# The gate of the second half: first layer on every partition, second layer as a row sum on DVE

## What is computed

```python
pooled = hidden_states.mean(axis=1)
h1 = jax.nn.relu(pooled @ gate_w1.T + gate_b1)          # 256 -> 64, per batch
base_act = jax.nn.sigmoid(h1 @ gate_w2.T + gate_b2)     # 64 -> 1
mod = jax.nn.sigmoid(safety_score[:, None] / TEMPERATURE)
strength = (base_act * mod * knob)[:, None, :]
...
return hidden_states + strength * response
```

## Time and profile before

| | |
|---|---|
| median of 3 runs | 1390.7 us (1389.85 to 1391.23) |
| profiled execution | 1390.32 us, its span 1388.2 us |
| busy: PE, DVE, ACT, POOL | 1335.7 (96%), 1066.6 (77%), 1077.6 (78%), 870.3 us (63%) |
| mean granted TensorE clock | 0.989 |
| part of the chain that ended last on PE | L1374 14%, L1361 14%, L1407 3%, L1385 1%, L1391 1%, L1396 1% |

### The profile page before, as it was taken

How to read it: one execution, slowest core, us unless ns; L and a number is a source line. 1 busy time by engine, 2 the same in 40 slices (tenths; PEclk the granted TensorE clock), 3 DMA queues, 4 the chain that set the end, 5 groups by cost and what they waited for, 6 DMA issues and landing times. The chain is left out here.

```text
span 1388.2 us, 39650 instructions
## 1 busy us (share of the span) xinstructions
PE 1335.7 (96%) x11998; PEld 1126.6 (81%) x11998; DVE 1066.6 (77%) x3539; ACT 1077.6 (78%) x2696; POOL 870.3 (63%) x874
## 2 busy tenths in 40 slices
PE   3899999999999999999999998799999999999997
PEld 3677777777777777777777776499999999999997
DVE  3787787777777877887777777577888888787875
ACT  0788888888888888888888887677777777777773
POOL 3989989999999998998998997222122122222210
PEclk9999999999999999999999999989999999999999
DMA  7656555565565564564654671001111111101000
GB/s 229 211 165 200 170 185 188 167 197 177 168 206 167 176 208 155 189 202 150 200 192 154 223 225 33 26 29 32 45 30 32 44 30 38 37 30 45 30 24 32
DMA packets 182766, 175.01 MB, mean 126 GB/s; under 512 B 15648, under 2 KB 182208, under 8 KB 182720
## 3 DMA queue, kind: packets, MB, share of 16 engines
q1 hardware_dynamic: 182720, 174.42, 39.5%
HBM read 157.63 MB, written 16.78 MB: 126 GB/s over the span
## 5 line engine op out<-in xcount | busy, mean ns | idle before, releaser
L423 POOL TENSOR_TENSOR ring<-ring,maskv 128x1024 f32<-128x1024 f32 x256 | 600.0, 2371 | 14.9 <-DMA ring<-in_fside 7.6
L885 ACT ACTIVATE ring<-ring,nmax 128x256 f32<-128x256 f32 x1024 | 453.0, 502 | 28.4 <-DVE nmax L599 28.4
L599 DVE CUSTOM_DVE_ANT_0 ring<-bank,ring 128x256 f32<-128x256 f32 x1024 | 373.1, 418 | 91.2 <-PE bank L1150 74.9
L890 ACT ACTIVATE pT<-bank 128x512 f32<-128x512 f32 x416 | 239.5, 592 | 101.6 <-PE bank L1165 101.5
L1165 PE MATMUL bank<-ident,ring 128*128 128x128 f32 x2048 | 293.5, 279 | 1.4 <-ACT pT L890 1.1
L1165 PEld LDWEIGHTS bank<-ident,ring 128*128 128x128 f32 x2048 | 232.3, 143 | 70.7 <-issue 47.8
L1020 ACT ACTIVATE work<-bank,b1t 128x256 f32<-128x256 f32 x256 | 107.5, 475 | 117.7 <-PE bank L1361 117.7
L1361 PE MATMUL bank<-hT_high,w_high 128*128 128x256 f32 x512 | 154.4, 302 | 4.2 <-DVE hT_rest L771 4.2
L1150 PE MATMUL bank<-work 32*128 32x256 f32 x2048 | 148.3, 404 | 5.2 <-DVE nmax L599 5.2
L1374 PE MATMUL bank<-w_high,gT_high 128*128 128x256 f32 x512 | 148.1, 289 | 0.0
L455 POOL TENSOR_SCALAR vpeb<-mvb 128x2 f32<-128x2 f32 x32 | 6.1, 191 | 226.5 <-DVE mvb L686 226.2
(11 more groups left out here) (158 smaller groups left out, 2724.3 us busy)
## 6 DMA issues: line engine op xcount, KB each, us to landing
ring<-in_fside SPq DMA_DIRECT2D x128, 1024.0 KB, 7.5
xt<-in_x SPq DMA_DIRECT2D x32, 256.0 KB, 3.1
x_d<-x2s SPq DMA_DIRECT2D x32, 256.0 KB, 7.7
work<-x_d SPq DMA_DIRECT2D x32, 256.0 KB, 2.7
out<-pT SPq DMA_DIRECT2D x32, 256.0 KB, 2.2
mk<-in_mask SPq DMA_DIRECT2D x32, 64.0 KB, 6.5
w<-in_W SPq DMA_DIRECT2D x2, 1024.0 KB, 10.5
wada<-in_W_ada SPq DMA_DIRECT2D x1, 512.0 KB, 4.3
```

The source lines that it names most:

```text
L423: nc.gpsimd.tensor_tensor(v, v, m, ALU.add).then_inc(s_masked, 1)
L599: nc.vector.tensor_tensor_reduce(out=v, in0=score_ps[h % HG][:, qt], in1=v, scale=-1.0, scalar=ROW_MAX_NEG, op0=ALU.add, op1=ALU.min, accu ...
L885: nc.scalar.activation(v, v, ACT.Exp, bias=nmax[:, b.par, h, qt:qt + 1], scale=-1.0).then_inc(s_exp, 1)
L890: nc.scalar.activation(pT[:, h % (2 * HG)], tp_ps[h % 2], ACT.Copy).then_inc(s_pta, 1)
```

## The change

Both layers of the gate give their result on all 128 partitions. The first layer now takes `pooled`, a column repeated to 128x128, as weights and moves the 64 columns of `gw1`: h1 lies along a row, the same row on every partition. DVE adds the bias (`gate_hidden`), and a second DVE instruction (`gate_sum`) applies relu, multiplies with the row `gw2` and sums along the row into `zsum`. `gate_z` on TensorE and `gate1` on ACT are gone. `gb1` and `gw2` are loaded as rows on every partition. On TensorE `up_pair(b, 1)` now stands ahead of `y_transpose`, and `hid_transpose` waits for h1 instead of z before it overwrites bank 6.

```diff
-gb1 = sb("gb1", [GW, 1]); gw2 = sb("gw2", [GW, 1])
+gb1 = sb("gb1", [P, GW]); gw2 = sb("gw2", [P, GW])
-h1 = sb("h1", [GW, 1])
+h1 = sb("h1", [P, GW]); h1w = sb("h1w", [P, GW]); zsum = sb("zsum", [P, 1])
...
-            (gb1[:], gate_b1.rearrange("(p a) -> p a", a=1)), (gw2[:], gate_w2T), ...
+            (gb1[:], gate_b1.partition_broadcast(P)), (gw2[:], gate_w2T.rearrange("p a -> (p a)").partition_broadcast(P)), ...
...
+            def gate_hidden(b):
+                dve.wait_ge(s2_h1p, b.n + 1)
+                nc.vector.scalar_tensor_tensor(h1[:], bank[6][:, 0:GW], 1.0 / S, gb1[:], ALU.mult, ALU.add).then_inc(s2_h1, 1)
+
+            def gate_sum(b):
+
+                dve.wait_ge(s2_h1, b.n + 1)
+                if b.i is not None or b.off >= 1:
+                    dve.wait_ge(s2_z, b.n)
+                dve.nop(nofuse=True)
+                nc.vector.scalar_tensor_tensor(h1w[:], h1[:], 0.0, gw2[:], ALU.max, ALU.mult, accum_out=zsum[:]).then_inc(s2_zs, 1)
...
                 if tail2:
+                    gate_hidden(b.plus(-2))
+                    gate_sum(b.plus(-2))
                     rsp_out(b.plus(-2))
...
-            def gate1(b):
-                act.wait_ge(s2_h1p, b.n + 1)
-                nc.scalar.activation(h1[:], bank[6][0:GW, 0:1], ACT.Relu, bias=gb1[:], scale=1.0 / S).then_inc(s2_h1, 1)
-
             def gate2(b):
-                act.wait_ge(s2_zp, b.n + 1)
+                act.wait_ge(s2_zs, b.n + 1)
                 if b.i is not None or b.off >= 1:
                     act.wait_ge(s2_str, b.n)
-                nc.scalar.activation(gth[:], bank[6][:, 8:9], ACT.Tanh, bias=gb2h[:], scale=0.5).then_inc(s2_z, 1)
+                nc.scalar.activation(gth[:], zsum[:], ACT.Tanh, bias=gb2h[:], scale=0.5).then_inc(s2_z, 1)
...
             def hid_transpose(b):
                 pe.wait_ge(s2_hid, b.n + 1)
                 if b.i is not None or b.off >= 1:
-                    pe.wait_ge(s2_z, b.n)
+                    pe.wait_ge(s2_h1, b.n)
...
             def gate_h1(b):
                 pe.wait_ge(s2_hidf, b.n + 1)
                 for c in range(DC):
-                    ins = mm(bank[6][0:GW, 0:1], gw1[:, c], pooled[:, c:c + 1], start=(c == 0), stop=(c == DC - 1))
+                    ins = mm(bank[6][:, 0:GW], pooled[:, c:c + 1].to_broadcast([P, P]), gw1[:, c], start=(c == 0), stop=(c == DC - 1))
                 ins.then_inc(s2_h1p, 1)
-
-            def gate_z(b):
-                pe.wait_ge(s2_h1, b.n + 1)
-                mm(bank[6][:, 8:9], h1[:].to_broadcast([GW, P]), gw2[:], start=True, stop=True).then_inc(s2_zp, 1)
...
                 if main:
                     up_pair(b, 0)
+                    up_pair(b, 1)
                     if n is None or n + 1 < B:
                         y_transpose(b.plus(1))
-                if main:
-                    up_pair(b, 1)
                 if tail2:
                     gate_h1(b.plus(-2))
...
-                if tail2:
-                    gate_z(b.plus(-2))
```

More of the change, by code:

```diff
@@ L138, in attention_block_kernel @@
         scr = sb("scr", [P, B]); modh = sb("modh", [P, B]); modt = sb("modt", [P, B])
-        gw1 = sb("gw1", [P, DC, GW]); gb1 = sb("gb1", [GW, 1]); gw2 = sb("gw2", [GW, 1]); gb2 = sb("gb2", [P, 1]); gb2h = sb("gb2h", [P, 1])
+        gw1 = sb("gw1", [P, DC, GW]); gb1 = sb("gb1", [P, GW]); gw2 = sb("gw2", [P, GW]); gb2 = sb("gb2", [P, 1]); gb2h = sb("gb2h", [P, 1])
         uv = sb("uv", [P, 2, DC, R]); ucol = sb("ucol", [P, 2, DC]); gsb = sb("gsb", [P, 2, R]); gii = sb("gii", [P, 2])
@@ L197, in attention_block_kernel @@
         fin = carve(2, QT, D)
-        pooled = sb("pooled", [P, DC]); h1 = sb("h1", [GW, 1]); gth = sb("gth", [P, 1]); strg = sb("strg", [P, 2])
+        pooled = sb("pooled", [P, DC]); h1 = sb("h1", [P, GW]); h1w = sb("h1w", [P, GW]); zsum = sb("zsum", [P, 1]); gth = sb("gth", [P, 1]); strg = sb("strg", [P, 2])
         st6b = sb("st6b", [P, QT, 6]); mvb = sb("mvb", [P, 2, QT, 2]); vpeb = sb("vpeb", [P, QT]); rstdb = sb("rstdb", [P, QT]); mnegb = sb("mnegb", [P, QT]); nmrb = sb("nmrb", [P, QT])
@@ L229, in attention_block_kernel @@
         s2_yt = sem("s2_yt"); s2_hT = sem("s2_hT"); s2_up = sem("s2_up"); s2_th = sem("s2_th"); s2_u = sem("s2_u"); s2_ua = sem("s2_ua"); s2_w = sem("s2_w"); s2_wl = sem("s2_wl"); s2_hf = sem("s2_hf"); s2_hl = sem("s2_hl"); s2_gh = sem("s2_gh"); s2_gl = sem("s2_gl"); s2_hidf = sem("s2_hidf"); s2_hidl = sem("s2_hidl"); s2_m = sem("s2_m"); s2_ml = sem("s2_ml"); s2_g = sem("s2_g"); s2_dn = sem("s2_dn")
-        s2_hid = sem("s2_hid"); s2_hidp = sem("s2_hidp"); s2_hidT = sem("s2_hidT"); s2_r = sem("s2_r"); s2_h1p = sem("s2_h1p"); s2_h1 = sem("s2_h1"); s2_zp = sem("s2_zp")
+        s2_hid = sem("s2_hid"); s2_hidp = sem("s2_hidp"); s2_hidT = sem("s2_hidT"); s2_r = sem("s2_r"); s2_h1p = sem("s2_h1p"); s2_h1 = sem("s2_h1"); s2_zs = sem("s2_zs")
         s2_z = sem("s2_z"); s2_str = sem("s2_str"); s2_rs = sem("s2_rs"); s2_fin = sem("s2_fin")
@@ L251, in attention_block_kernel @@
             (gw1[:], gate_w1T.rearrange("(c p) n -> p c n", p=P)),
-            (gb1[:], gate_b1.rearrange("(p a) -> p a", a=1)), (gw2[:], gate_w2T), (gb2[:], gate_b2.partition_broadcast(P)),
+            (gb1[:], gate_b1.partition_broadcast(P)), (gw2[:], gate_w2T.rearrange("p a -> (p a)").partition_broadcast(P)), (gb2[:], gate_b2.partition_broadcast(P)),
             (respT[:], resp_wT),
@@ L1076, in body2 @@
                     gT_high(b, 0)
-                if tail2:
-                    gate1(b.plus(-2))
                 if main:
```

## The result

The changed kernel took 1373.65 us (median of 4 executions, 1371.87 to 1374.12) against 1390.85 us (4 executions): ratio 0.9876, 95% interval 0.9861 to 0.9891. A later series of 4 gave a median of 1372.8 (1371.27 to 1374.35), ratio 0.9867 (0.9837 to 0.9896), against a median of 1389.6 for the kernel before in that series. So it is faster by some 17 us, near the forecast of 1372.0 and inside its range. The profiled execution took 1371.87 us (span 1369.7).

What follows compares the result with a forecast made beforehand. TensorE's own instruction stream was taken as the bound, 14.71 us a pass. Gains 29 x 0.60 = 17.4, pass 31 0.5, pass 0 0.6, end 0.2 sum to 18.7 us: 1372.0 us, range 1369 to 1378.

Steps and rivals of the forecast that it cites:

- gate_z, 0.50 us: Gate's second layer on TensorE: removing it gains 0.50 us a pass, though its records take 0.31 on the chain.
- gate_h1, 0.41 us from the Gram product: Gate's first layer on TensorE: four records at the Gram product's 0.1025 each, 0.41 us; gain 0.10 with the transposes.
- rival 1: Gate_h1's edges stay, caused by f32 with a wait, not shape; gate_h1 costs 0.59, time 1377.3 us; chance 0.12.
- slow exit back to the ordinary products: TensorE after y's transposes: a delay before ordinary products resume, taken as already contained in the transposes' 0.44 us.
- The loads and the edges: Gate_h1 on TensorE: four records grow from 0.33 to 0.41 us, and the edges of 0.18 vanish with the shapes.
- a sum 3.8 us worse: Gate_h1's weight loads: by the skill's rule four loads cost 0.21 us more instead of 0.08, worsening the whole sum.
- Pass 0, 0.6 us: Start of the second half: second up pair ends 0.85 us sooner with the order exchanged; counted as 0.6 us.
- DVE hidden: New gate_hidden and gate_sum, 0.75 us of DVE's queue, fit narrowly in 0.89 us: nothing on the path.
- it costs 1:1 once it is over 1.6 us: DVE's new work: beyond room of 0.89 + 0.7 us, each added us lengthens the path by as much.
- Rival 2: DVE's work not fully hidden: 2.0 us per pass stalls hid transposes 0.4; gain 7, about 1385 us; chance 0.06.
- rival 3: Slower than before: gate_sum holds up DVE; needs 2.3 us for both instructions; 2.5 gives 1398 us; chance 0.03.
- The end, 0.2 us: Last output: strength can follow rsp_out directly, 0.6 us behind, without gate_z and its tanh; gain 0.2 us.

Runs made afterwards that it cites:

- 64-row run: Changed kernel plus one unused f32 product where gate_z stood, 64 rows by 128 columns of weights, one column moving: 1386.39 us, passes 14.66 and 14.67 us.
- the two runs on the order: Changed kernel with y's transposes back between the up pairs: 1372.71 us; kernel before with only those two calls exchanged: 1389.81 us.
- full-shape run: Changed kernel plus one unused f32 product where gate_z stood, 128x128 weights, one column moving: 1378.34 us, passes 14.38 us.
- the two runs: Changed kernel with two more 128x512 sums on DVE ahead of rsp_out: 1379.07 us; with four more: 1403.99 us.
- the run with the order undone: Changed kernel with y's transposes back between the first and second up pair: 1372.71 us, ratio to before 0.9875.
- the last run: Changed kernel with pooled and gw1 rounded to fp32r, making the gate's first layer single-pass products: 1364.96 us, ratio to before 0.9814.

## Why the prediction was right

**What bounds it.** Right: the chain is TensorE's stream before and after, and every experiment on that stream moved the pass by just the price of the instructions edited.

**gate_z, 0.50 us.** Right to 0.01: the 64-row run puts it back for 0.50.

**gate_h1, 0.41 us from the Gram product.** Right in mechanism, a little off in size. The full shape takes the late loads away, so rival 1 (the edges belong to f32 and the wait) falls. The term that was mis-sized is "4 x 0.1025 = 0.41": it measured 0.45 behind the transposes, 0.44 alone. The 0.1025 came from the starts of products, and the recorded start of a product is not at a fixed distance from its load: 0.11 us behind it in an ordinary stream, 0.02 behind a small group (load 1111.40, product 1111.42). The Gram product's own loads would have given 0.11:

```profile
319.18 0.97 PEld L1116 LDWEIGHTS bank<-uv,ucol 128*128 128x128 f32 x8
```

(0.97 - 0.19) / 7 = 0.111, and four of these are 0.445. The "slow exit back to the ordinary products" is the same matter: the step of 0.20 us between the first two products behind a small group stands in the starts of the products alone, while their loads follow at 0.11. So no exit was there to be contained in the transposes' 0.44 (four loads of 0.11) or to be merged by the order; the two runs on the order show it. 0.89 us instead of 0.85 makes a pass 14.16 instead of 14.11, and 29 steps together 16.0 us shorter (426.68 against 410.64) instead of 17.4.

**The loads and the edges.** Here two errors nearly cancelled, which is luck. The forecast let the records grow by 0.08 us and the edges shrink by 0.18. The loads grew by 4 x (0.11 - 0.057) = 0.21 us, and the edges that went were 0.28 of the old 0.51. The Trainium skill's rule on LDWEIGHTS (TensorE: Matmul & The Clock Gate), the number of columns over 1.2 in ns whatever the rows in use, makes an estimated 107 ns for 128 columns and 53 for 64; the trace agrees, with loads 0.11 and 0.057 us apart and 0.11 for 64 rows of 128 columns. What the prediction drew from it, a sum 3.8 us worse, left out that the edges were larger too. That the number of moving columns does not show was right: 0.11 a record with 1 column (the full-shape run), 32 (the Gram product) and 64.

**Pass 0, 0.6 us.** Right: 0.6 to 0.8 less.

**DVE hidden.** Right, with 0.42 us to spare, but its terms were mis-sized. The new work took 0.50 us instead of 0.75, because the second instruction follows 0.35 behind the first and rsp_out 0.15 behind that. The room ahead of the transposes, forecast as 0.7, was 0.42: the forecast counted up to their piece of the chain (1117.85), not to their first load. So "it costs 1:1 once it is over 1.6 us" was wrong twice. The room, 0.89 + 0.44, was 1.3 us; and beyond it 0.50 + 1.20 = 1.70 us would cost 0.4 at 1:1 and 0.50 + 2.40 = 2.90 would cost 1.6, where 0.19 and 0.95 were measured. Rival 2's 2.0 us and rival 3's 2.5 us did not occur (rival 2's sum, a gain of 7 us, gives 1384, not "about 1385"). Rival 3's point of decision, 2.3 us, lies between the two runs: 1.70 us left the kernel at 1379.07 us, 2.90 at 1403.99.

**The end, 0.2 us.** The last output starts right behind rsp_out, as said: from the end of the last response to the start of fin_out 1.05 us (1365.28 to 1366.33) against 1.28 (1383.47 to 1384.75). Not foreseen: in pass 32 TensorE has waited for ACT, and there the new gate_h1 is the dearer one. From its start to the end of the down product behind it, on the chain, it is 3.58 us in the run with the order undone against 3.45 before, both with a down product of 3.1 us or less, and 5.08 and 5.10 in the two profiles of the changed kernel against 4.94 in the second of before, all with one of 4.3 us or more. So 0.13 to 0.16 us of the 0.23 is given back.

**The sum.** From the first up pair of the second half to the end it was 486.2 us in both profiles of before, and 468.7 and 469.1 after: 17.1 to 17.5 us against the 18.7 forecast. Of it 16.0 are the 29 passes, 0.5 pass 31, 0.6 to 0.8 pass 0 and 0.1 the end. That the two profiles of before agree is chance: one lost 1.6 us in pass 1, the other 1.5 in pass 32. Both profiles of the changed kernel lost theirs in pass 32 too, so the comparison is fair to some tenths.

## What to carry to other kernels

Where one engine's stream is the bound, read the price of a small instruction from the start of the last ordinary one before it to the second one after it, not from its duration or its share of the chain: gate_z was 0.31 us on the chain and cost 0.50. Read the price of one record from the starts of the weight loads. A product with few columns is cheaper on the full array, with operands repeated to fill it, than in its natural small shape in the middle of full-shape ones, as long as the group is short. By an estimate from the loads here the visit's 0.28 us is made up for by 64-column loads at 0.28 / (0.11 - 0.057), about 5 records; the gate had 4 and won 0.06 us, and no run tried a longer group. And a product whose result serves every partition can save the next one: that was nine tenths of the gain. When work moves to another engine, count the room before the wait that it could delay: here 0.99 us of idle time took 0.50 us of new work.

## What the runs showed of the hardware that was not expected

- A single plain f32 product costs 0.22, 0.40 or 0.50 us in the stream by shape alone (128x128, 128 rows with 64 columns, 64 rows with 128 columns).
- Behind that lie two terms: 0.11 us a record for its load of 128 columns (0.057 for 64), and 0.28 to 0.29 us for going to another shape and back. The number of moving columns (1, 32, 64) did not show, nor did the precision, other than by the count: a plain f32 product has two records, a single-pass one has one, and halving them in the last run took 0.23 us from a pass.
- The step of 0.20 instead of 0.12 us between the first two ordinary products behind a small group is no cost of its own. It stands behind plain f32 groups and behind the single-pass gate_h1 alike (1110.50 to 1110.70 in the last run), and the loads there follow without a gap.
- A stall caused by DVE's queue grew by less than the work added beyond the room (0.19 us a pass for 0.34, 0.95 for 1.54, with 0.44 + 0.42 us of room left in the changed kernel): the longer pass also lengthens the time in which DVE waits for its next input. That reading is argued from the order of the waits; only the sizes are shown.
- Beside the change, TensorE's clock decides some 1.5 us of an execution in two places where TensorE has just idled. The 24 products of pass 32 took 3.06 us at a granted clock of 1.00 (1369.5 to 1373.5 us) in the first profile of before, and 4.55 and 4.40 at 0.66 (1367 to 1372 and 1350 to 1355 us) in the second of before and the first of the changed kernel. In the last of these the clock was at 0.50, its 1.2 GHz level, from 1350.7 to 1353.0 us. TensorE had idled 1.74 us before gate_h1 in all three. In pass 1, entered after 2.0 to 2.1 us of idle time, the first profile of before lost 1.6 us at a granted clock of 0.79 from 912 to 920 us, where the second had 1.00. So the idle time alone does not decide it. This is part of why executions of the same kernel spread by about 3 us.
